# Another order of the setup work in the first attention group of a one-core Trainium2 kernel

## The reference

```python
x = x + tanh(g_xattn[0]) * xattn(layernorm(x), ctx, ctx, w_qs, w_ks, w_vs, w_proj, b_proj)
x = x + tanh(g_ffn[0])   * ffn(layernorm(x), gate_w, w1, w2)
# xattn: 16 heads of 64; qh, kh, vh = projections of q, k, v
attn = softmax(einsum('hblk,hbmk->hblm', qh, kh))
out  = einsum('hblm,hbmk->hblk', attn, vh) * qh        # then @ w_proj.T + b_proj
# ffn: logits = x @ gate_w.T; top 2 of 8; softmax of the two logits; silu(x @ w1) @ w2
```

## Time and profile before

| | |
|---|---|
| median of 3 timed runs | 798.28 us |
| the profiled execution's own time | 796.72 us |
| its span, first to last instruction | 794.6 us |
| TensorE busy with matmuls | 740.1 us (93%) |
| VectorE, ScalarE, GpSimd busy | 610.5, 382.5, 417.3 us |
| mean granted TensorE clock | 0.987 of full |

### The profile page before, as it was taken

How to read it: one execution, slowest core, us unless ns; L and a number is a source line. 1 busy time by engine, 2 the same in 40 slices (tenths; PEclk the granted TensorE clock), 3 DMA queues, 4 the chain that set the end, 5 groups by cost and what they waited for, 6 DMA issues and landing times. The chain is left out here.

```text
span 794.6 us, 23823 instructions
## 1 busy us (share of the span) xinstructions
PE 740.1 (93%) x8020; PEld 615.9 (78%) x8021; DVE 610.5 (77%) x1305; ACT 382.5 (48%) x680; POOL 417.3 (53%) x380
## 2 busy tenths in 40 slices
PE   4979999999999999987799998999999999999991
PEld 2657777676767777755798887899999999999991
DVE  6668889999898989794777778877777777777760
ACT  3566776767666676653344432333333333333330
POOL 3124454757676666645434475645555555555542
PEclk9999999999999999999899999999999999999997
DMA  8543242627272534423688866433333333333321
GB/s 268 160 108 132 80 161 92 234 81 265 74 255 93 208 113 175 139 100 87 207 217 229 233 161 125 76 54 47 48 52 50 49 46 53 50 50 47 51 32 20
DMA packets 94104, 93.74 MB, mean 118 GB/s; under 512 B 59216, under 2 KB 77840, under 8 KB 94032
## 3 DMA queue, kind: packets, MB, share of 16 engines
q1 hardware_dynamic: 32400, 65.89, 25.0%
q0 software_dynamic: 13392, 18.03, 13.0%
q10 hardware_dynamic: 48240, 8.87, 7.0%
HBM read 53.76 MB, written 37.95 MB: 115 GB/s over the span
## 5 line engine op out<-in xcount | busy, mean ns | idle before, releaser
L1399 PE MATMUL h_ps<-bx_h,w_now 128*128 128x128 f16 x2272 | 195.4, 220 | 12.5 <-DVE bx_l L1536 12.4
L1412 PE MATMUL pair_ps<-weights,ht_h 128*128 x1136 | 190.7, 273 | 2.5 <-DVE ht_l L1550 1.8
L1399 PEld LDWEIGHTS h_ps<-bx_h,w_now 128*128 128x128 f16 x2272 | 153.0, 98 | 17.3 <-DVE bx_l L1536 15.2
L1399 PE MATMUL h_ps<-bx_l,w_now 128*128 128x128 f16 x1136 | 157.0, 220 | 0.0
L1412 PE MATMUL pair_ps<-weights,ht_l 128*128 x568 | 154.9, 273 | 0.0
L1656 POOL DMA_INDIRECT out<-y,meta x71 | 144.3, 2032 | 15.7 <-issue 8.8
L1221 POOL TENSOR_TENSOR r_l<-r,r_h 128x512 f16<-128x512 f32 x64 | 74.3, 1161 | 104.8 <-ACT r_h L835 104.8
L1655 POOL TENSOR_TENSOR wait_mark<-wait_mark 128x1 f32<-128x1 f32 x71 | 40.3, 567 | 163.3 <-DMA out<-y,meta 101.9
L1412 PEld LDWEIGHTS pair_ps<-weights,ht_h 128*128 128x128 f16 x1136 | 110.0, 97 | 18.2 <-issue 3.6
L1475 ACT ACTIVATE y<-pair_ps,meta 128x256 f32<-128x256 f32 x71 | 33.6, 473 | 175.6 <-DVE bx L1525 75.8
L1548 DVE CAST ht_h<-hid 128x1024 f16<-128x1024 f32 x71 | 49.4, 696 | 73.2 <-ACT hid L1468 73.2
(11 more groups left out here) (260 smaller groups left out, 1326.8 us busy)
## 6 DMA issues: line engine op xcount, KB each, us to landing
stage<-in_w SPq DMA_DIRECT2D x16, 1024.0 KB, 8.7
w_split<-split SPq DMA_DIRECT2D x14, 1024.0 KB, 6.1
weights<-w_split SPq DMA_DIRECT2D x14, 1024.0 KB, 5.9
rows<-records ACTq DMA_DIRECT2D x268, 32.0 KB
xin<-in_x SPq DMA_DIRECT2D x8, 512.0 KB, 4.9
x_even<-in_x SPq DMA_DIRECT2D x4, 512.0 KB, 3.6
x_odd<-in_x SPq DMA_DIRECT2D x4, 512.0 KB, 3.6
out<-x_even SPq DMA_DIRECT2D x4, 512.0 KB, 2.7
```

The costliest lines, as they stand in the source:

```text
L1399: last = nc.tensor.matmul(h_ps[r % 2][:, c, :], w1_now[:, r % 2, s, k * F + c * P:k * F + c * P + P], xt[:, r % 2, k, :], start=(j == 0 an ...
L1412: last = nc.tensor.matmul(y_ps[r % 2], ht[:, r % 2, c, :], weights_at(e, s, WN // 2 + c * D, D).rearrange("p o n -> p (o n)"), start=(c == ...
```

## The change

All of it is in group 0. Two tables now say in which step a K projection and a quarter of the weight transposes are done.

```diff
+    K_AT = ((0, 1, 2), (3,), (4,), (5,), (6,), (7,), (), ())
+    WP_AT = ((), (0,), (1,), (2, 3), (), (), (), ())
...
     def pieces(g, p):
 
         if isinstance(g, int) and g == 0:
-            return range(3 * (p - 5), min(3 * (p - 4), WC)) if p >= 5 else ()
+            return {3: (0, 1), 4: (2,), 5: (3,), 6: (4, 5), 7: (6, 7)}.get(p, ())
         return (p,)
...
+    def k_bank(p):
+        return {1: pt_ps[:, :], 2: ot_ps[:, 1, :]}.get(p, job_ps[:, :])
+
+    def k_batches(p, h):
+        return k_bank(p)[h * DK:(h + 1) * DK, 0:B * M].rearrange("p (b m) -> p b m", m=M)
...
@@ transpose_wp @@
-            after(pe, wp_lo, part)
+            after(pe, wp_lo, part - 1)
+            pe.wait_ge(k_placed, 2 * len(K_AT[0]))
...
-                    last = nc.tensor.transpose(ot_ps[:, 0, j * D + c * P:j * D + (c + 1) * P], wp_sb[:, c, o:o + P], ident[:, :])
+                    last = nc.tensor.transpose(ot_ps[:, part % 2, j * D + c * P:j * D + (c + 1) * P], wp_sb[:, c, o:o + P], ident[:, :])
...
@@ project_k @@
-            after(pe, k_placed, 2 * p)
-            if p == 6:
-                pe.wait_ge(xt_lo, KD + 1)
-            if p == 7:
-                pe.wait_ge(xt_lo, 2 * KD)
+            if p >= len(K_AT[0]):
+                pe.wait_ge(k_placed, 2 * p)
             for k in range(KD):
-                last = nc.tensor.matmul(job_ps[:, 0:B * M], wk_cols[:, k, p * P:(p + 1) * P],
+                last = nc.tensor.matmul(k_bank(p)[:, 0:B * M], wk_cols[:, k, p * P:(p + 1) * P],
...
@@ small_job, p == 5, g == 0 @@
-                    pe.wait_ge(k_placed, 2 * p + 2)
+                    pe.wait_ge(k_placed, 2 * NP)
...
@@ step of ScalarE @@
             if p == 4 and has_next(g):
-                ln1_apply(g + 1, 1 - k, range(TG if first else TG // 2))
-            if p == 5 and has_next(g) and not first:
+                ln1_apply(g + 1, 1 - k, range(TG // 2))
+            if p == 5 and has_next(g):
                 ln1_apply(g + 1, 1 - k, range(TG // 2, TG))
```

More of the change, by code:

```diff
@@ L404, in k_place @@
         return kb[h * DK:(h + 1) * DK, :, p, h * M:(h + 1) * M]
-    def k_batches(h):
-        return job_ps[h * DK:(h + 1) * DK, 0:B * M].rearrange("p (b m) -> p b m", m=M)
+    def k_bank(p):
+        return {1: pt_ps[:, :], 2: ot_ps[:, 1, :]}.get(p, job_ps[:, :])
+    def k_batches(p, h):
+        return k_bank(p)[h * DK:(h + 1) * DK, 0:B * M].rearrange("p (b m) -> p b m", m=M)
     def v_place(vb, part, u):
@@ L694, in small_job @@
                 pe.wait_ge(xt_lo, 2 * g + 3)
-                if isinstance(g, int) and g == 0:
-                    pe.wait_ge(k_placed, 2 * p + 2)
                 x_transpose(g + 1, 1, job_ps)
@@ L709, in step @@
             if isinstance(g, int) and g == 0:
-                project_k(p)
+                for v in K_AT[p]:
+                    project_k(v)
             if pairs_back >= 1:
@@ L717, in step @@
                 transpose_probs(n - 4, back(4)[2])
-            if isinstance(g, int) and g == 0 and p < 4:
-                transpose_wp(p)
+            if isinstance(g, int) and g == 0:
+                for part in WP_AT[p]:
+                    transpose_wp(part)
             if isinstance(g, int) and g == 0 and 1 <= p <= B:
@@ L797, in place_k @@
                 act.wait_ge(k_zeroed, 1)
-            nc.scalar.copy(k_place(kb, p, 0), k_batches(0)).then_inc(k_placed, 1)
+            nc.scalar.copy(k_place(kb, p, 0), k_batches(p, 0)).then_inc(k_placed, 1)
         def place_v(part):
@@ L809, in split_wp @@
             act.wait_ge(wp_tp, part + 1)
-            nc.scalar.mul(wp_h[:, 2 * part:2 * part + 2, :], ot_ps[:, 0, :].rearrange("p (q d) -> p q d", q=2), WS).then_inc(wp_hi, 1)
+            nc.scalar.mul(wp_h[:, 2 * part:2 * part + 2, :], ot_ps[:, part % 2, :].rearrange("p (q d) -> p q d", q=2), WS).then_inc(wp_hi, 1)
         def copy_q(n, p):
@@ L879, in step @@
             if first:
-                place_k(p)
+                for v in K_AT[p]:
+                    place_k(v)
             if p == 2 and known(g, 2):
@@ L884, in step @@
                 probs_out(n - 4, (p - 4) % NP)
-            if first and p < 4:
-                split_wp(p)
+            if first:
+                for part in WP_AT[p]:
+                    split_wp(part)
             if first and 1 <= p <= B:
@@ L996, in place_k @@
                 dve.wait_ge(k_zeroed, 1)
-            nc.vector.tensor_copy(k_place(kb, p, 1), k_batches(1)).then_inc(k_placed, 1)
+            nc.vector.tensor_copy(k_place(kb, p, 1), k_batches(p, 1)).then_inc(k_placed, 1)
         def split_wp(part):
             dve.wait_ge(wp_hi, part + 1)
-            nc.vector.scalar_tensor_tensor(wp_l[:, 2 * part:2 * part + 2, :], ot_ps[:, 0, :].rearrange("p (q d) -> p q d", q=2), WS,
+            nc.vector.scalar_tensor_tensor(wp_l[:, 2 * part:2 * part + 2, :], ot_ps[:, part % 2, :].rearrange("p (q d) -> p q d", q=2), WS,
                                            wp_h[:, 2 * part:2 * part + 2, :], ALU.mult, ALU.subtract).then_inc(wp_lo, 1)
```

## The result

| | before | after |
|---|---|---|
| median of timed runs, same chip | 796.47 us (17 runs) | 793.15 us (17 runs) |
| ratio after to before | | 0.995, 95% interval 0.9933 to 0.9968 |
| profiled execution, its own time | 796.72 us | 793.26 us |
| its span | 794.6 us | 791.1 us |
| mean granted clock | 0.987 | 0.984 |

The change makes the kernel faster by 0.5%: the interval is 2.5 to 5.3 us of 796. A second series of the same kernel gave 0.9956 (0.9935 to 0.9976). The time 792.9 us was forecast and 793.15 came, but the gain was forecast as 5.35 us. The two agree only because the kernel before was timed at 796.47 us here, 1.8 us under the median of the three runs that were known. So the interesting number is the missing 2 us of gain.

What follows compares the result with a forecast made beforehand. TensorE sets the pace, with stalls and low clock in group 0. Delay +1.10, new wait +2.12, old wait -0.67 and -7.90 after the transposes gain 5.35 us: 798.28 to 792.9 us, range 790.7 to 794.2 (796.0 with A and B).

Steps and rivals of the forecast that it cites:

- The stalls of steps 6 and 7 go: TensorE's xt_l waits of 2.90 and 1.35 us vanish; transposes to group 1 shrink from 18.08 to 10.18 us.
- The new wait: Step 5, before the row transposes: TensorE stands 2.12 us until ScalarE finishes xn, the old 0.67 us included.
- Two more K projections in step 0: Two projections come and one transpose quarter leaves, so step 1 starts 1.05 us later, bounds 0.85 to 1.30.
- The hole in step 2: The scores' 0.39 us wait in step 2 absorbs part of the 1.05 us delay, leaving 0.66 us.
- Pieces 0 and 1 cost nothing: Two weight pieces on ScalarE in step 3, 1.10 us, are covered by its 1.13 us wait before step 4's V copies.
- rival B: ScalarE jammed: pieces 0 and 1 uncovered, step 5's wait 3.2 us and the clock falls; 795.3 us, chance 0.12.
- Nothing is lost behind group 0: After group 0 TensorE sets the pace, so the 5.35 us saved in group 0 shifts all that follows.
- C: Gain lost after group 0 because something there is tied to transfers, not TensorE; 798.3 us, chance 0.07.
- D: Piece 0 in step 3 waits for its late load, stopping ScalarE; 800.8 us for a landing at 46, chance 0.04.
- The clock: Step 6's low clock behind the 2.90 us wait goes, saving 1.27 us; no fall costed at step 5's wait.
- starting up: Steps 6 and 7: 0.64 us of starting up after the stalls is saved, part of the 7.90 us.
- A: The clock falls at step 5's new wait as well, the rest of the gain stays; 794.2 us, chance 0.17.

Runs made afterwards that it cites:

- k_only: Changed kernel with only the moved K projections, weight-transpose quarters and banks; normalisation full in step 4, weight pieces as before the change; 791.06 us, ratio 0.9947.
- tanh_late: Kernel before with only the two small tanh-gain loads moved behind the loads of the next rows and expert 0; 795.93 us, ratio 1.0001.
- ln_full: Changed kernel with the normalisation of all four row tiles back in step 4 on ScalarE; 793.95 us, ratio 0.9983.
- pieces_only: Kernel before with only expert 0's weight pieces spread as in the change (two in step 3, one in 4, one in 5); 796.14 us, ratio 0.9998.
- before, third: Kernel before run unchanged a third time for its trace; step 6 took 11.91 us, group 1 started at 63.62 us.

## Why the prediction was right or wrong

Right: direction and range, and the time by luck of the median. Point by point:

- **The stalls of steps 6 and 7 go.** They did, in all three traces of after. Without a fall, the transposes to group 1 take 58.23 - 48.04 = 10.19 us; 10.18 was forecast.
- **The new wait, 2.12 us in front of the transposes.** 2.29, 2.30 and 2.29 us, ended by `xn`. The forecast let VectorE's K 7 copy end 0.8 us ahead of `xn`; it began at 47.02 in after, and was in time.
- **Two more K projections in step 0, +1.05 us.** Step 1 started at 19.85 in the mean of three (20.43, 19.26, 19.85) against 18.63 (19.11, 18.07, 18.70): +1.22 us, inside the bounds of 0.85 and 1.30. The second traces, in which step 0 runs at full speed from its first K projection on, show the size: the first q matmul of step 1 starts at 19.47 instead of 18.18, +1.29 us, which is the 1.74 us of the two projections less 0.44 for the quarter, and not less the 0.89 that the quarter took in the first trace. How slow step 0 was differed from one execution to the next.
- **The hole in step 2 takes 0.39 us back.** It took about 0.2. Step 2 is 5.39 to 5.46 us long before, and 5.20 with nothing in its way; step 1 became 0.10 us longer as well (20.43 to 25.42, against 19.11 to 24.00). TensorE was ready for the transposes 1.51 us later in the third pair (45.57 against 44.06) where 1.10 was forecast; in the first pair it was 1.61 us, with the late DMA in it, and in the second 2.27, with the late rows.
- **Pieces 0 and 1 cost nothing.** ScalarE still waited 0.99 us for the V projection of step 4. Right, and rival B with it is out.
- **Nothing is lost behind group 0.** 317.7 to 317.8 us from group 1 to the experts in each trace but k_only's, which has 318.2. Rivals C and D fell.
- **The clock.** This is the step that failed. The sum took 1.27 us of clock out of the kernel before as if the fall belonged to it, and put none into the kernel after. Of the 0.64 us of "starting up" another 0.14 belonged to the fall; 0.49 stayed without one. In fact both waits bring the clock down in some executions and not in others: two of three traces of before (three of four with tanh_late, whose wait is the same 2.90 us), and two of three of after (three of four with ln_full's 2.34). Without a fall the gain from the transposes on is (60.82 - 44.15) - 10.19 = 6.48 us, not 7.90. Less the delay of 1.5 us, the new wait of 2.30, plus the old one of 0.68, that is 3.4 us; the falls on both sides about cancel. The missing 2.0 us of gain are thus 1.4 of clock, 0.4 of a larger delay and 0.2 of a longer wait. The mean start of group 1 moved from 62.58 to 59.40, 3.2 us, and the timed medians by 3.3 and 3.7.

The Trainium skill ("TensorE: Matmul & The Clock Gate", section "What's actually happening") says that the window for the clock runs freely against the kernel, so that the moment of a change varies. The repeats agree: the same gap, once with a clock of 1.00 and once with 0.50. I quoted this in the prediction and then gave a fall at the new wait 0.29 (rivals A and B), and didn't apply it to the kernel before at all, although it holds for both sides.

Of the change's four parts, two together carry the gain: the new places of the K projections and of the quarters. k_only has them without the others; the two were not run apart. pieces_only gives nothing. The piece in step 4 is by itself enough for the new wait (2.34 us in ln_full, 2.35 in pieces_only); that halving the normalisation alone would make one as well was not run.

## What to carry to other kernels

When a trace shows a slow clock behind a wait, don't book its cost as a sure gain: read several executions of the kernel before, and weigh the fall on both sides. A gap that passed at full clock in one trace is no bound either: the 2.44 us one fell in eight of 14. When work is moved into a gap of an in-order engine, look at what stands behind it there on both engines that share it: a weight piece on ScalarE held VectorE for 3.11 us and with it a copy that TensorE waited for. Read landmarks in the trace (start of a stage) when the time of the whole varies by more than the change.

## What the runs showed of the hardware

- The fall of the clock isn't set by the length of the wait alone. Waits of 2.29 us (twice), 2.34 and 2.90 us (three times) were followed by a clock of 0.50; others of 2.30, 2.35 and 2.90 us were not. The 2.44 us wait at the end of attention had a fall in eight of 14 traces. The waits of 0.19 to 0.68 us in front of the transposes never had one. The cost in group 0 was 1.4 us (before), 1.66 (after) and 2.2 net (before, third, and tanh_late); at the end of attention it was nothing.
- In the six traces of group 0 with a fall, its moment (48.25 to 50.0) came later the later the first K projection of step 0 had ended (18.35 to 18.98). In after it came 1.3 us after the wait was over.
- The SP queue held the issue of the tenth DMA of the start for 3.77 to 6.99 us, both when it was the first tanh load (11 traces) and when it was the rows' load (3).
- From the first expert matmul to the end took 412.4 to 416.8 us, 2.3 us apart in three traces of the same kernel. A wait of 2.0 to 3.0 us on `bx_l` near 505 us comes in some of them. Its cause wasn't looked into.
